# The output product of a recurrent mixer as two stacked float32r products instead of one fp32 product

## The chip, the cores and the metric

One core of a Trainium2 chip runs the whole program. The metric is the device time in microseconds of one execution. In what follows PE is the matrix engine (TensorE), DVE the vector engine, ACT the scalar engine, POOL GpSimd, SP the engine that issues most DMAs.

## The reference, cut to what matters

One transformer-like layer on x of shape (2, 1024, 512), with adaptive scales and shifts from a small product (mod). First a recurrent mixer (64 states), then a mixture of 32 experts (4 per token) with a shared expert of 1408 columns, both with a residual.

```python
h = layernorm(x) * (1 + ca) + sa
x_cat = jnp.roll(h, -512, axis=1)
x_shift = jnp.einsum('btd,ed->bte', x_cat, Wts) * g + h * (1.0 - g)
xn = layernorm(x_shift) * ln_w + ln_b
k = jnp.einsum('btd,sd->bts', xn, Wk)
v = jnp.einsum('btd,sd->bts', xn, Wv)
wkv = jnp.exp(-jnp.exp(time_first) * jax.nn.sigmoid(k)) * v
states[t] = states[t - 1] * jnp.exp(time_decay) + wkv[t]     # a scan over 1024 rows
out = jnp.einsum('bts,ds->btd', states, Wo)                  # the output product
x = x + ga * out
h2 = layernorm(x) * (1 + cb) + sb
x = x + gb * ffn(h2)        # router, top 4 of 32 experts, shared expert
```

## The kernel before, in words

The 2048 rows stand as NT = 16 tiles of 128 rows, eight for each of the two batches; a group is GT = 4 tiles (512 rows). Every engine has its own program, written out by hand in Python loops; the engines meet only in semaphores (`then_inc`, `wait_ge`), so an instruction that waits holds up everything that stands behind it on its engine.

The part in question is one loop, `for t in range(STEPS)`, of 22 steps, which each engine writes for itself. In step t:

- PE turns (transposes) the next tile of normalized rows (`turn(("h", t + 1))`), computes `mixer(t)`, a product of 12 float32r matmuls of 128x512 (L1640), then `project(t - 5)`, the output product of tile t - 5 (L1662), then turns `xn` and `h2` rows, and at t = 4, 8, 12, 16 computes `keys_values(g)` for group g = t / 4 - 1 (L1653). In steps 9 and 17, `project` stands at the step's end, in step 13 behind the first piece of shared-expert work. From step 10 on, pieces of the shared expert's first two chunks (L1690, L1702) fill in, and `router(g)` (L1673) at t = 9, 13, 17, 21.
- ACT takes turned tiles out of PSUM (hT rounded to float32r at L737, `xnT` at L742, `h2T` at L752), normalizes rows (L770, L787), prepares `kE` and `vV` for the scan (`decay_factor`, L810 to L813) and rounds the shared expert's operands (`xsH`, L860; `prodH`, L874).
- DVE adds and takes statistics (`mix_front` at L1151, `residual_sum` at L1164), forms the low halves of split operands (`h_lo` at L1058, `xsL` at L1214, `prodL` at L1224), and at the end of steps 4, 8, 12, 16 multiplies and scans (`kv_scan`, L1184 and L1187).
- POOL computes the reciprocal roots of the variances (`rsx`, `rsh`) and the row sums and scalings (L623 to L642).

A split operand is a float32 value as a rounded float32r part (H) and the rest (L), so that a sum of float32r products, H·H, H·L and L·H, gives nearly the float32 product. `mixer` and the shared expert do it so. `project` does not: it is one plain fp32 product of 64 rows (the 64 states) by 512 columns, which the compiled program runs as two matmul instructions. Its stationary operand is `states`, 64x512 for each of two groups in turn; its moving operand is `woT[:, b, :]`, the output weights scaled by the gate `ga` of batch b. Those are made once, in step 4: DVE scales `Wo` in eight instructions (`derive`, L1144) into `ho[:, 1, :]`, PE turns them (`("wo", b)`), ACT copies them out of PSUM (L728).

`project(t)` waits for `st_ok` of its group, given by the scan. The next group's scan takes the last state of the group before out of `states`. The "rows" turn of step 5 carries modulation vectors to HBM by way of `rowT`. The semaphores `t_full` and `t_taken` of the three PSUM banks for turns order PE against whoever takes a turned tile.

## Time and profile before

| what | value |
| --- | --- |
| runs, us | 720.56, 728.2, 723.08; median 723.08 |
| the profiled execution | 720.62 us, its span 718.8 us |
| mean granted TensorE clock | 0.976 |
| busy: PE, DVE, ACT, POOL | 672.5, 365.5, 288.6, 184.4 us |
| matmul instructions of the project product, L1662 | 32, 589 ns each |
| DMA | 118.27 MB, 165 GB/s on average |

The profile's times count from the start of the span. An idle time in square brackets is what an instruction's engine waited before it, with the instruction that released it. "issue" means that nothing in the profile is seen to have been waited for. A shape such as 64*128 64x512 gives the stationary operand (rows by columns) and the moving one. The mixer loop runs from about 28 to 235 us; behind it come routing, the experts and the rest of the shared expert.

### The profile page before, as it was taken

The page shows a single profiled execution, that of the slowest core. Times are in us where ns is not written, and L with a number is a line of the kernel's source. Part 1 is how long each engine was busy: PE and PEld are TensorE (multiplying, and loading weights), DVE is VectorE, ACT ScalarE, POOL GpSimd, SP SyncE. Part 2 cuts the span into 40 slices and gives each one's busy share as a digit, 9 for nine tenths or more (in the row PEclk, how much of TensorE's full clock was granted, in tenths as well). Part 3 has the DMA queues.
Part 4 walks back from the last instruction along what each step waited for, and adds up shares of the span by engine and source line. Part 5 has one row for each costly group of instructions (what it writes and reads, how often), then busy time and mean ns, then how long its engine had stood idle before and what let it go on. Part 6 is the DMA issues. An engine that isn't in the chain of part 4 may idle for free.

```text
span 718.8 us, 8895 instructions
## 1 busy us (share of the span) xinstructions
PE 672.5 (94%) x3218; PEld 467.9 (65%) x3218; DVE 365.5 (51%) x714; ACT 288.6 (40%) x552; POOL 184.4 (26%) x174
## 2 busy tenths in 40 slices
PE   4898788999998899998999899999999999999997
PEld 3665456768576667887665566666666666667875
DVE  3768759679687887763124223122122243225755
ACT  3444775656656543323234224233232343323231
POOL 1254465554627200000112122222221222120000
PEclk9799987999999999999999999999999999999999
DMA  7760200000223006305777877778899787816311
GB/s 276 243 238 1 76 15 30 16 30 18 85 77 116 29 1 232 134 1 206 267 235 231 291 229 261 249 234 282 270 324 338 239 273 258 284 23 234 117 50 69
DMA packets 50295, 118.27 MB, mean 165 GB/s; under 512 B 6904, under 2 KB 11084, under 8 KB 50252
## 3 DMA queue, kind: packets, MB, share of 16 engines
q1 hardware_dynamic: 45388, 109.31, 43.0%
q0 software_dynamic: 4864, 8.40, 5.4%
q8 instruction: 26, 0.43, 0.2%
q14 instruction: 17, 0.14, 0.1%
HBM read 100.87 MB, written 18.91 MB: 167 GB/s over the span
## 4 chain that ended last, share of the span: by engine, by line
PE 61%; DVE 5%; DMA 3%; ACT 2%; issue 2%; POOL 2%; SPq 0%; DVEq 0%; ACTq 0%; POOLq 0%
PE bank L1690 28%; PE bank L1702 11%; PE bank L1745 11%; PE bank L1762 6%; DMA egu<-in_L_ffn_Wu_dram 1%; PE bank L1733 1%; ACT xsH L860 1%; DMA xg<-h_rows,slot_tok 1%; PE bank L1793 1%; PE bank L1751 1%; DVE xres L1260 1%; DVE prodL L1224 1%; POOL ho L634 1%; DVE prod L1222 1%; POOL xres L642 1%
## 5 line engine op out<-in xcount | busy, mean ns | idle before, releaser
L1690 PE MATMUL bank<-xsH,wguH 128*128 128x512 f32 x352 | 144.1, 409 | 1.5 <-DVE xsL L1214 1.1
L1690 PE MATMUL bank<-xsL,wguH 128*128 128x512 f32 x352 | 138.9, 394 | 0.0
L1690 PE MATMUL bank<-xsH,wguL 128*128 128x512 f32 x352 | 138.6, 394 | 0.0
L1690 PEld LDWEIGHTS bank<-xsH,wguH 128*128 128x128 f32 x352 | 67.0, 190 | 25.5 <-issue 10.9
L1222 DVE TENSOR_TENSOR prod<-bank,silu 128x512 f32<-128x512 f32 x38 | 26.2, 690 | 111.2 <-PE bank L1690 87.7
L1745 PE MATMUL bank<-egu,xeT 128*64 128x352 f32 x512 | 79.3, 462 | 3.1 <-DMA egu<-in_L_ffn_Wu_dram 2.6
L1702 PE MATMUL bank<-wdH,prodH 128*128 128x512 f32 x176 | 73.7, 419 | 6.4 <-DVE prodL L1224 4.2
L692 POOL DMA_INDIRECT expert_sums<-ye,slot_to x32 | 49.4, 1543 | 115.7 <-DMA expert_sums<-ye,slot_to 91.5
L1690 PEld LDWEIGHTS bank<-xsL,wguH 128*128 128x128 f32 x352 | 66.9, 190 | 14.8
L1690 PEld LDWEIGHTS bank<-xsH,wguL 128*128 128x128 f32 x352 | 66.8, 190 | 13.2 <-issue 0.7
L699 POOL DMA_INDIRECT xg<-h_rows,slot_tok x16 | 16.8, 1053 | 219.8 <-DVE slot_w L1368 90.0
L874 ACT ACTIVATE prodH<-prod 128x512 fp32r<-128x512 f32 x38 | 24.0, 632 | 114.8 <-DVE prod L1222 114.8
L1702 PE MATMUL bank<-wdH,prodL 128*128 128x512 f32 x176 | 68.9, 391 | 0.0
L1702 PE MATMUL bank<-wdL,prodH 128*128 128x512 f32 x176 | 68.8, 391 | 0.0
L1745 PEld LDWEIGHTS bank<-egu,xeT 128*64 128x64 f32 x512 | 36.2, 137 | 42.2 <-issue 35.4
L868 ACT ACTIVATE silu<-bank 128x512 f32<-128x512 f32 x44 | 26.3, 598 | 71.9 <-PE bank L1690 70.5
L1248 DVE TENSOR_TENSOR xres<-ytmp,xres 128x512 f32<-128x512 f32 x44 | 30.0, 691 | 45.9 <-ACT ytmp L911 45.6
L1640 PE MATMUL bank<-wtsH,hT 128*128 128x512 f32 x128 | 49.1, 447 | 4.5 <-DVE mx L1151 3.1
L1702 PEld LDWEIGHTS bank<-wdH,prodH 128*128 128x128 f32 x176 | 33.1, 188 | 23.8 <-issue 7.4
L1214 DVE TENSOR_TENSOR xsL<-h2T,xsH 128x512 fp32r<-128x512 f32 x64 | 44.9, 746 | 4.8 <-ACT xsH L860 4.7
L1383 DVE TENSOR_TENSOR eprod<-bank,esilu 128x352 f32<-128x352 f32 x16 | 8.4, 525 | 75.0 <-ACT esilu L884 75.0
L1762 PE MATMUL bank<-ed,epT 128*64 128x512 f32 (+1 forms) x192 | 44.8, 600 | 0.8 <-issue 0.8
(222 smaller groups left out, 1019.8 us busy)
## 6 DMA issues: line engine op xcount, KB each, us to landing
egu<-in_L_ffn_Wg_dram SPq DMA_DIRECT2D x32, 704.0 KB, 6.0
egu<-in_L_ffn_Wu_dram SPq DMA_DIRECT2D x32, 704.0 KB, 7.5
ed<-in_L_ffn_Wd_dram SPq DMA_DIRECT2D x32, 512.0 KB, 5.3
h2T<-in_L_wmod_dram SPq DMA_DIRECT2D x6, 1024.0 KB, 8.9
ed<-in_L_ffn_Wd_dram SPq DMA_DIRECT2D x32, 192.0 KB, 6.3
h_rows<-ho SPq DMA_DIRECT2D x16, 256.0 KB, 2.0
expert_sums<-ye SPq DMA_DIRECT2D x16, 256.0 KB, 8.8
out_dram<-xres SPq DMA_DIRECT2D x16, 256.0 KB, 2.2
```

What stands on the lines that cost most here:

```text
L692: gp.indirect_dma_start(sums_dram[:, :], bass.IndirectOffsetOnAxis(slot_to[0:n, e, j:j + 1], axis=0), ye[0:n, :], None, bounds_check=B * T ...
L699: gp.indirect_dma_start(xg[:, :], None, h2_dram[:, :], bass.IndirectOffsetOnAxis(slot_tok[:, j:j + 1], axis=0)).then_inc(xg_in, 16)
L868: a.activation(silu[:, :], gB[:, :], ACT.Silu).then_inc(silu_ok, 1)
L874: a.activation(prodH[f][:, :], src[:, :], ACT.Copy).then_inc(phi_ok, 1)
L1214: v.tensor_tensor(xsL[:, c, :], h2T[:, g, c, :], xsH[:, c, :].bitcast(F32), ALU.subtract).then_inc(xlo_ok, 1)
L1222: v.tensor_tensor(to[:, :], uB[:, :], silu[:, :], ALU.mult).then_inc(prod_ok, 1)
L1248: v.tensor_tensor(xres[:, i, :], taken(p, g, m)[:, :], xres[:, i, :], ALU.add).then_inc(x_acc, 1)
L1640: ins = mm.matmul(s_bank[k][:, :], l[:, c, :], r[:, c, :], start=(n == 0), stop=(n == 3 * C - 1))
L1690: ins = mm.matmul(bk[:, :], l[f][:, w, c, :], r[:, c, :], start=(k == 0), stop=(k == 3 * C - 1))
L1702: ins = mm.matmul(dB[m % 2][:, :], l[f][:, m * P:(m + 1) * P], r[f][:, :], start=(f == 0 and k == 0), stop=(f == nf - 1 and k == 2))
L1745: ins = mm.matmul(bk[side, 0:F], xeT[:, c, side], egu[:, e, w, c, :], start=(c == 0), stop=(c == C - 1))
L1762: ins = mm.matmul(eyB[side, :], epT[0:n, c, side], ed[0:n, e, c, :], start=(c == 0), stop=(c == len(FC) - 1))
```

## The change

The states of a group are kept in `kE`, where the scan now writes in place. ACT rounds them into rows 0 to 63 of a new tile `sHL` (`states_hi`); DVE puts the rest into rows 64 to 127 (`states_lo`), and only that gives `st_ok`. The output weights stand twice, in rows 0 to 63 and again in 64 to 127: DVE's scaling writes each 64 columns twice, PE turns 128 columns instead of 64, ACT rounds the result into `woH`, and DVE puts the rest into `woL` (`wo_lo`). `project` is then two float32r products of 128 rows: `sHL` by `woH`, and `sHL` by `woL`, so all four cross terms are summed. The last state of a group goes to `wcol[:, 3:4]` with a copy at even groups. `rowT` loses its own memory and lies in `vV`, so ACT's "rows" copy waits for the first scan, and `decay_factor(1)` for the DMA out of it.

```diff
-            states_all = sb("states", [P, 2, GW], F32, pa)
-            woT = sb("woT", [S, B, H], F32, pa)
+            with ExitStack() as opening:
+                partial = sb("partial", [P, 2, GW], F32, opening)
+            sHL = sb("sHL", [P, 2, GW], F32R, pa)
+            woH = sb("woH", [P, B, H], F32R, pa)
+            woL = sb("woL", [P, B, H], F32R, pa)
...
-        woS = ho[:, 1, :].rearrange("p (c b s) -> p c b s", c=C, b=B)
+        woS = [ho[:, 1 + b, :] for b in range(B)]
+        rowT = vV[0:B * KINDS * C, 0:P]
...
                     elif kind == "wo":
-                        a.activation(woT[:, t[1], :], src[0:S, :], ACT.Copy).then_inc(t_taken[k], 1)
+                        a.activation(woH[:, t[1], :], src[:, :], ACT.Copy).then_inc(wo_hi, 1)
                     elif kind == "rows":
-                        a.activation(rowT[:, :], src[0:B * KINDS * C, 0:P], ACT.Copy).then_inc(t_taken[k], 1)
+                        act.wait_ge(st_full, 1)
+                        a.activation(rowT, src[0:B * KINDS * C, 0:P], ACT.Copy).then_inc(t_taken[k], 1)
...
+                    if g == 1:
+                        act.wait_ge(vrows_out, 16)
...
+                def states_hi(g):
+                    act.wait_ge(st_full, g + 1)
+                    a.activation(sHL[0:S, g % 2, :], kE[:, :], ACT.Copy).then_inc(st_hi, 1)
...
                     for q in before_mixer(t):
                         take(q)
+                    if scan_group(t - 1) is not None:
+                        states_hi(scan_group(t - 1))
...
                         for c in range(C):
-                            v.tensor_scalar(woS[:, c, b, :], woN[:, c, :], dcol[:, b, K_GA, c:c + 1], None, ALU.mult).then_inc(wo_scaled, 1)
+                            v.tensor_scalar(woS[b][:, c * P:(c + 1) * P].rearrange("p (a s) -> p a s", a=2),
+                                            woN[:, c:c + 1, :].to_broadcast([P, 2, S]), dcol[:, b, K_GA, c:c + 1], None,
+                                            ALU.mult).then_inc(wo_scaled, 1)
...
                     link(v.tensor_tensor(kE[:, :], vV[:, :], kE[:, :], ALU.mult))
-                    if g:
-                        dve.wait_ge(st_ok, g)
-                    v.tensor_tensor_scan(states[:, g % 2, :], wcol[:, 0:1].to_broadcast([S, GW]), kE[:, :],
-                                         states[:, 0, GW - 1:GW] if g % 2 else 0.0, ALU.mult, ALU.add).then_inc(st_ok, 1)
+                    v.tensor_tensor_scan(kE[:, :], wcol[:, 0:1].to_broadcast([S, GW]), kE[:, :],
+                                         wcol[:, 3:4] if g % 2 else 0.0, ALU.mult, ALU.add).then_inc(st_full, 1)
+                    if g % 2 == 0:
+                        dve.wait_ge(st_full, g + 1)
+                        link(v.tensor_copy(wcol[:, 3:4], kE[:, GW - 1:GW]))
+
+                def states_lo(g):
+                    dve.wait_ge(st_hi, g + 1)
+                    v.tensor_tensor(sHL[S:2 * S, g % 2, :], kE[:, :], sHL[0:S, g % 2, :].bitcast(F32),
+                                    ALU.subtract).then_inc(st_ok, 1)
+
+                def wo_lo(b):
+                    k, _ = turn_at[("wo", b)]
+                    dve.wait_ge(wo_hi, b + 1)
+                    v.tensor_tensor(woL[:, b, :], bank[k][:, :], woH[:, b, :].bitcast(F32), ALU.subtract).then_inc(t_taken[k], 1)
...
                     if 1 < t + 1 < NT:
                         h_lo(t + 1)
+                    if scan_group(t - 1) is not None:
+                        states_lo(scan_group(t - 1))
...
                     if t == 4:
                         derive_gb()
+                        wo_lo(0)
+                        wo_lo(1)
...
-                    mm.matmul(s_bank[k][:, :], states[:, g % 2, i * P:(i + 1) * P], woT[:, t // BT, :],
-                              start=True, stop=True).then_inc(s_full[k], 1)
+                    mm.matmul(s_bank[k][:, :], sHL[:, g % 2, i * P:(i + 1) * P], woH[:, t // BT, :], start=True, stop=False)
+                    mm.matmul(s_bank[k][:, :], sHL[:, g % 2, i * P:(i + 1) * P], woL[:, t // BT, :],
+                              start=False, stop=True).then_inc(s_full[k], 1)
```

DVE before, at the end of step 4 and the start of step 5, behind the first scan (`dcol` are vectors for the gate of the second half, `hT` is the low half of the next mixer operand, `neg` and `nb` are small vectors, `mx` is the sum with the mixer product):

```order
L1127 TENSOR_TENSOR dcol<-tmpc 128x4x2
L1132 RECIPROCAL dcol<-dcol 128x4x2
L1058 TENSOR_TENSOR hT<-bank,hT 128x512
L1051 TENSOR_TENSOR neg<-mv,neg_one 128x4
L1053 TENSOR_TENSOR nb<-neg,rs 128x4
L1151 TENSOR_TENSOR mx<-bank,mx 128x512
```

DVE now, the same place:

```order
L1135 TENSOR_TENSOR dcol<-tmpc 128x4x2
L1140 RECIPROCAL dcol<-dcol 128x4x2
L1209 TENSOR_TENSOR woL<-bank,woH 128x512 x2
L1066 TENSOR_TENSOR hT<-bank,hT 128x512
L1203 TENSOR_TENSOR sHL<-kE,sHL 64x512
L1059 TENSOR_TENSOR neg<-mv,neg_one 128x4
L1061 TENSOR_TENSOR nb<-neg,rs 128x4
L1161 TENSOR_TENSOR mx<-bank,mx 128x512
```

Two subtractions for the output weights (`woL`) stand ahead of `hT`, and the low half of the states (`sHL`) behind it, all of them ahead of `mx`.

DVE before, at the third scan, from the end of step 12 into step 13 (`kE` is the input of the scan, `st` a statistic of `mx`):

```order
L1184 TENSOR_TENSOR kE<-vV,kE 64x512
L1187 SCALAR_TENSOR_TENSOR states<-wcol,kE 64x512
L1058 TENSOR_TENSOR hT<-bank,hT 128x512
L1151 TENSOR_TENSOR mx<-bank,mx 128x512
L1153 BN_STATS st<-mx 128x6
```

DVE now, the same place:

```order
L1194 TENSOR_TENSOR kE<-vV,kE 64x512
L1195 SCALAR_TENSOR_TENSOR kE<-wcol,kE 64x512
L1199 COPY wcol<-kE 64x1
L1066 TENSOR_TENSOR hT<-bank,hT 128x512
L1203 TENSOR_TENSOR sHL<-kE,sHL 64x512
L1161 TENSOR_TENSOR mx<-bank,mx 128x512
L1163 BN_STATS st<-mx 128x6
```

A one-column copy follows the scan (at the first and third scan alone), and the low half of the states stands between `hT` and `mx` (at the first three scans; at the last there is no `hT` and no `mx` behind it).

ACT before, around the last scan, at the end of step 16 and in step 17 (`kE` and `vV` prepare the scan, `h2T` is the router's operand, `xsH` the shared expert's):

```order
L810 ACTIVATE kE<-bank,kvbias 64x512
L811 ACTIVATE vV<-bank,kvbias 64x512
L813 ACTIVATE kE<-kE,wcol 64x512
L752 ACTIVATE h2T<-bank,dcol 128x128 x4
L860 ACTIVATE xsH<-h2T 128x512 x4
```

ACT now:

```order
L812 ACTIVATE kE<-bank,kvbias 64x512
L813 ACTIVATE vV<-bank,kvbias 64x512
L815 ACTIVATE kE<-kE,wcol 64x512
L819 ACTIVATE sHL<-kE 64x512
L754 ACTIVATE h2T<-bank,dcol 128x128 x4
L866 ACTIVATE xsH<-h2T 128x512 x4
```

The rounded half of the states, which waits for DVE's scan, now stands ahead of `h2T` and `xsH`. The line numbers of the changed kernel run up to 26 higher than those of the kernel before.

## Rows read from the trace of the kernel before

**Rows 1.** The page's first part: busy time of each engine, share, instructions.
```profile
PE 672.5 (94%) x3218; PEld 467.9 (65%) x3218; DVE 365.5 (51%) x714; ACT 288.6 (40%) x552; POOL 184.4 (26%) x174
```

**Rows 2.** Timeline, PE, step 11: start us, us, line, operation, count, [idle before].
```profile
134.10 0.39 PE L1640 MATMUL bank<-wtsH,hT 128*128 128x512 f32 x1
134.41 1.12 PE L1662 MATMUL bank<-woT,states 64*128 64x512 f32 x2
135.47 0.50 PE L1690 MATMUL bank<-xsH,wguH 128*128 128x512 f32 x1
135.80 0.39 PE L1690 MATMUL bank<-xsH,wguL 128*128 128x512 f32 x1
136.03 0.40 PE L1690 MATMUL bank<-xsL,wguH 128*128 128x512 f32 x1
```

**Rows 3.** Timeline, DVE: end of step 4, start of step 5.
```profile
63.65 1.40 DVE L1144 TENSOR_SCALAR ho<-ho,dcol 128x64 f32<-128x64 f32 x8
...
66.92 0.68 DVE L1184 TENSOR_TENSOR kE<-vV,kE 64x512 f32<-64x512 f32 x1
...
67.64 1.22 DVE L1187 TENSOR_TENSOR_SCAN states<-wcol,kE 64x512 f32<-64x512 f32 x1
...
68.78 0.13 DVE L1130 COPY modc<-bank 128x8 f32<-128x8 f32 x1
...
70.10 0.64 DVE L1058 TENSOR_TENSOR hT<-bank,hT 128x512 fp32r<-128x512 f32 x1
```

**Rows 4.** Timeline, PE: project product of step 5.
```profile
68.96 1.09 PE L1662 MATMUL bank<-woT,states 64*128 64x512 f32 x2
```

**Rows 5.** Timeline, three engines, steps 6 to 8: the relay from row to row.
```profile
78.55 0.68 DVE L1151 TENSOR_TENSOR mx<-bank,mx 128x512 f32<-128x512 f32 x1
...
94.56 0.29 ACT L776 ACTIVATE nbh<-negh,rsh 128x1 f32<-128x1 f32 x1 [1.05 <-POOL rsh L606]
...
97.93 0.69 DVE L1058 TENSOR_TENSOR hT<-bank,hT 128x512 fp32r<-128x512 f32 x1 [3.81 <-ACT hT L737]
```

**Rows 6.** Timeline, steps 8 to 10, DVE and then PE.
```profile
108.27 1.24 DVE L1184 TENSOR_TENSOR kE<-vV,kE 64x512 f32<-64x512 f32 x1 [4.30 <-ACT kE L813]
...
121.10 3.79 DVE L1214 TENSOR_TENSOR xsL<-h2T,xsH 128x512 fp32r<-128x512 f32 x4 [0.78 <-ACT xsH L860]
...
123.74 0.52 PE L1690 MATMUL bank<-xsH,wguH 128*128 128x512 f32 x1 [0.69 <-DVE xsL L1214]
```

**Rows 7.** Windows: us, PE, PEld, DVE, ACT, POOL busy, PEclk, DMA, GB/s.
```profile
124.00:128.00 4.00, 4.00 (x14) 3.07 (x14) 3.80 (x10) 0.71 (x2) 0.00 (x0) 0.57 0.17 63
128.00:149.00 21.00, 21.00 (x99) 15.82 (x98) 13.59 (x31) 11.60 (x25) 13.13 (x13) 1.00 0.07 26
```

**Rows 8.** Timeline, steps 12 to 16: DVE, then PE twice.
```profile
157.63 1.22 DVE L1187 TENSOR_TENSOR_SCAN states<-wcol,kE 64x512 f32<-64x512 f32 x1
...
158.95 1.09 PE L1662 MATMUL bank<-woT,states 64*128 64x512 f32 x2 [0.16 <-issue]
...
190.67 0.50 PE L1702 MATMUL bank<-wdH,prodH 128*128 128x512 f32 x1 [0.89 <-DVE prodL L1224]
```

**Rows 9.** Timeline, step 17 to step 20: ACT, DVE, PE.
```profile
199.07 1.50 ACT L752 ACTIVATE h2T<-bank,dcol 128x128 f32<-128x128 f32 x4 [0.26 <-PE bank L1591]
200.66 2.20 ACT L860 ACTIVATE xsH<-h2T 128x512 fp32r<-128x512 f32 x4
...
201.32 2.50 DVE L1214 TENSOR_TENSOR xsL<-h2T,xsH 128x512 fp32r<-128x512 f32 x4 [0.48 <-ACT xsH L860]
205.01 0.69 DVE L1164 TENSOR_TENSOR xres<-bank,xres 128x512 f32<-128x512 f32 x1 [1.18 <-PE bank L1662]
...
224.79 0.50 PE L1702 MATMUL bank<-wdH,prodH 128*128 128x512 f32 x1 [1.37 <-DVE prodL L1224]
```

**Rows 10.** Groups by line, DVE: busy us, mean ns | idle before.
```profile
L1224 DVE TENSOR_TENSOR prodL<-prod,prodH 128x512 fp32r<-128x512 f32 x38 | 26.3, 692 | 26.5 <-ACT prodH L874 26.5
...
L1224 DVE TENSOR_TENSOR prodL<-silu,prodH 128x512 fp32r<-128x512 f32 x6 | 7.9, 1324 | 7.4 <-ACT prodH L874 7.4
```

More of the change, by code:

```diff
@@ L152, in build @@
             dcol = sb("dcol", [P, B, KINDS, C], F32, pa)
-            rowT = sb("rowT", [B * KINDS * C, P], F32, pa)
             tmpc = sb("tmpc", [P, 3, C, B], F32, pa)
@@ L181, in build @@
         rows = ho[0:24, 2, 2 * P:3 * P]
+        rowT = vV[0:B * KINDS * C, 0:P]
         kvN = mx[:, 1, :]
         kvT = mx[:, 2, :].rearrange("p (c m) -> p c m", c=C)
-        partial = states_all
-        states = states_all[0:S, :, :]
         LOT, NHOT = 8, 5
@@ L258, in build @@
          vef_ok, vex_ok, veh_ok, rsf_ok, rsx_ok, rsh_ok, dve_self, pool_self,
-         vrows_out, ab_in, cb_in, sb_in, rg_in, gate_in) = sems(
+         vrows_out, ab_in, cb_in, sb_in, rg_in, gate_in, wo_hi, st_full, st_hi) = sems(
              "rows_zero const_ok cols_in kv_in wo_in wr_in stage_in0 stage_in1 stage_in2 "
@@ L265, in build @@
              "vef_ok vex_ok veh_ok rsf_ok rsx_ok rsh_ok dve_self pool_self "
-             "vrows_out ab_in cb_in sb_in rg_in gate_in")
+             "vrows_out ab_in cb_in sb_in rg_in gate_in wo_hi st_full st_hi")
         (w_in, w_read, sg_exp, rb_ok, shift_ok, ex_ok, pos_full, mask_ok, scan_ok, route_ok,
@@ L500, in _ @@
                 turn_taken(sp, ("rows",))
-                sp.dma_start(rows_dram, rowT[:, :]).then_inc(vrows_out, 16)
+                sp.dma_start(rows_dram, rowT).then_inc(vrows_out, 16)
                 sp.wait_ge(vrows_out, 16)
@@ L779, in norm_out @@
                         act.wait_ge(wo_scaled, B * C)
-                    elif t == 1:
-                        turn_full(act, ("wo", 1))
-                    elif t == 2:
-                        act.wait_ge(part_full, len(VECTORS))
+                    elif t <= B:
+                        turn_full(act, ("wo", t - 1))
                     else:
@@ L1573, in turn @@
                         pe.wait_ge(wo_scaled, (t[1] + 1) * C)
-                        src, dst = [woS[:, c, t[1], :] for c in range(C)], dst[0:S, :]
+                        src = [woS[t[1]][:, c * P:(c + 1) * P] for c in range(C)]
                     else:
```

## The prediction

> **What bounds the kernel now.** I read the page's first part, then the timelines of PE and DVE side by side from 60 us to 240 us, since every touched instruction runs there. PE is busy 94% of the span [rows 1], which invites the conclusion that any time taken off PE comes off the kernel. For this stretch the reader should see that it is only sometimes so, and the waits tell where.
>
> Steps 4 to 9 (about 58 to 115 us) are a relay: DVE forms a row's statistics, POOL its rstd, ACT normalizes, ACT rounds the next hT, DVE subtracts, and only then does DVE take the next mixer product. in steps 7 and 8 ACT waits 1.05 us for POOL's rsh and DVE 3.81 us for ACT's hT [rows 5], and POOL had waited for DVE. PE follows: its products are ready before DVE takes them. At steps 8 to 10 the relay runs through ACT's kE into an unbroken DVE row (kE, the scan, hT, mx, xres, wguL, wdL, xsL), and PE waits 0.69 us for xsL [rows 6]. From 128 to 149 us PE is busy 21.00 of 21.00 us [rows 7]: here it is the bound. From the scan at 157.63 us DVE is again nearly unbroken, until PE waits 0.89 us for prodL at 190.67 [rows 8]. In steps 17 to 20 PE waits 1.37 us for a prodL [rows 9], which goes back over ACT and POOL to the DVE row that starts at 205.01 us. Behind 240 us nothing touched is left, so a shift there is carried to the end unchanged.
>
> **What leaves PE.** Sixteen project products of two fp32 passes each. In step 11 the last mixer product starts at 134.10 us and the first product behind the project at 135.47: 1.37 us, of which 0.23 is the mixer product's own step (135.80 to 136.03), leaving 1.14; the first product behind also takes 0.33 instead of 0.23 until its follower starts. So a project costs 1.24 us of PE's row [rows 2]. The two float32r products in its place are of the form whose step is 0.23 us, so 0.46 us, and 0.78 us is saved, if PE is the bound there. I take float32r over sHL and woH as the same form as the shared products over xsH and wguH (128 rows, 512 columns).
>
> "FP8 and Floating Point Precision" of the Trainium skill (TensorE Precision Notes) counts true fp32 as four passes. By it and the 0.23 us step of these rows the old product would be 0.92 us and the saving 0.46; the row shows 1.24, since the project also starts late and delays its follower, and the row decides.
>
> **What DVE gets**, each piece between instructions that the relay already waits for:
> - Step 4, scaling of Wo: eight instructions of 128 columns for eight of 64, which took 1.40 us, 0.18 each; one of 8 columns takes 0.13 [rows 3], so most is fixed. Between 0 and 1.4 us more; I take 0.3.
> - Two woL subtractions from PSUM, like the hT subtraction of 0.64 us [rows 3]: 1.3 us, in front of h_lo of step 5.
> - The copy of the last state at groups 0 and 2: about 0.13 us [rows 3], plus the wait for the scan's end where the follower used to overlap it: 0.3 us each, between 0.2 and 0.5.
> - Four states_lo, 64x512 with two inputs in SBUF, like kE: 0.68 us at 66.92, 1.24 at 108.27 [rows 3, 6]. I take 0.7, and 1.24 as the other end.
> - ACT gets four states_hi, like one xsH: a quarter of 2.20 us, 0.55 [rows 9]. DVE's states_lo waits for it.
>
> **Steps 4 and 5.** Scale 0.3, copy 0.3, woL 1.3, states_lo 0.7: 2.6 us more before DVE takes mixer product 5 (it stands right behind the hT of 70.10 us and two small ones [rows 3]). states_hi is hidden here under DVE's small instructions and woL. PE is hit too: project 0 started at 68.96 [rows 4] and now waits for states_lo, which ends near 73.5. Behind that wait stand mixer product 6 and the turn of xn 4; they come some 4 us late. DVE takes product 6 near 81.2 (78.55 plus 2.6 [rows 5]), and a late start at 75.6 with twelve products of 0.23 to 0.43 us ends between 78.6 and 81, so this stays hidden, if barely. I carry +2.6 through the relay to step 8; the projects of steps 5 to 8 give nothing, because PE waits after each.
>
> **Steps 8 to 10.** DVE's row gets states_lo, and before it the wait for ACT: st_full, 0.55 us of states_hi, then 0.7, of which hT hides 0.6. Net +0.9 before mx 9, and everything up to xsL at 121.10 is back to back. ACT's xnT and h2T also stand behind states_hi, but ACT waits for POOL's rstd just behind them, which has the same 0.9 us to come. The saved 0.78 of projects 4 and 5 only makes PE wait longer for xsL. +0.9.
>
> **Steps 11 and 12**: PE is the bound; two projects, 2 x 0.78 = -1.6.
>
> **Steps 13 to 16.** Copy 0.3, states_lo with its wait 0.9 less 0.1: +1.1 on DVE's row from 157.63 to 190.67. PE also waits for states_lo at project 8 (it started at 158.95, 0.1 us behind the scan [rows 8]): some +1.0 there. The four projects of steps 13 to 16 then save 3.1 us on PE, which turns the 0.89 us wait at 190.67 into about 3. +1.1.
>
> **Step 17.** states_hi now stands in front of h2T and xsH on ACT and waits for the scan's end at 200.84 (201.32 less the wait of 0.48), so xsH, which began at 200.66, begins near 203.0, and xsL, its pursuer, ends about 2.4 us later, near 206.2 instead of 203.8. (From 200.84: 0.55 of states_hi, then the 1.50 of h2T, which used to be done from 199.07 on.) DVE had waited 1.18 us for project 12 at 205.01 [rows 9]; that wait vanishes and the row starts at 206.2: +1.2. The later projects again only lengthen PE's wait.
>
> **Sum**: 2.6 + 0.9 - 1.6 + 1.1 + 1.2 = +4.2 us. The profiled execution took 720.6 us (718.8 of span, 1.8 around it), so 724.8 for it. It lies 2.5 us under the median 723.1 of the runs shown; from the median the forecast is 727.3.
>
> **Rivals.**
> - *PE decides everywhere* (faster). If the eleven projects from step 10 on all come off, and the DVE pieces fall in gaps: 11 x 0.78 = 8.6 us, 714.5. For it: PE's 94% [rows 1] and the gapless 21 us [rows 7]. Against: the three waits of PE for DVE in [rows 6, 8, 9], each at the end of a row to which DVE work is added. 0.08.
> - *The pieces are absorbed.* DVE is busy 51% overall [rows 1], and waits like 3.81 us [rows 5] look like room. If steps 4 to 8 absorb the 2.6: 723.1 + 4.2 - 2.6 = 724.7; if all is absorbed and PE's gain of 1.6 is left, 721.5. Against it: the waits are for ACT and POOL, which wait for DVE's earlier instruction, so the gap moves with it. 0.17.
> - *PE's clock* (slower). At 124 to 128 us the granted clock is 0.57 of full on average [rows 7], so mostly the 1.2 GHz level, where a product's step of 0.23 us about doubles, to 0.43; just before, PE had waited for xsL [rows 6]. The change makes PE wait more (4.5 us at step 5, 1.5 at 13, 3 at 16). Half clock costs nothing while PE waits anyway; it decides once two or three such stretches of 3.4 us fall where PE is the bound, as after 128 us [rows 7]: 1.7 us each, 3.4 to 5.1, so 730.7 to 732.4. 0.12.
> - *POOL holds DVE up* (slower). The same prodL takes 0.69 us late in the kernel and 1.32 beside POOL's row work [rows 10], so 1.24 for each states_lo: +0.5 x 4, 729.3. 0.13. "SBUF — State Buffer" of the Trainium skill (SBUF: two separate sides) says that a DVE instruction with two SBUF inputs and a GpSimd one exclude each other for a whole instruction; that speaks against this change, since states_lo is of that kind. By it each collision may cost a POOL instruction's whole length; the trace agrees in kind, with 1.32 for 0.69.
>
> **How the numbers follow.** The forecast, with sizes as above, has 0.50: 725 to 730. Predicted time: 727.3. Range 720 to 732: it takes in the absorbed case, POOL and the lower part of the clock case, and leaves out PE deciding everywhere and the worst of the clock. One per cent, 7.2 us, is about what a measurement can tell from no change: the three runs before lie 7.6 us apart. Faster by over 1% (under 715.8) 0.08, slower by over 1% (over 730.3) 0.16, within 0.76.
>
> **What the profile after would show.** Right: PE idle of 4 us or more before the first woH product, released by states_lo; project products of 0.39 us each; xsL and prodL still ending PE's waits, longer than before at 190 us; step 17's xsH behind states_hi. Wrong: mixer product 6 or xnT ending DVE's or ACT's waits in steps 6 and 7 (then step 5 costs over 2.6 us), no wait for prodL in step 16 (then DVE was no bound and the projects count), or states_lo near 1.24 us. What would overturn the sign is slack in the relay that I have not seen.

## The result and the profile after

The changed kernel takes 732.5 us (median of 4 runs, 731.1 to 734.6) where the kernel before takes 723.6 beside it on the same chip: ratio 1.0137, 95% interval 1.0105 to 1.0169. It is slower by 9.9 us by that ratio; the forecast was +4.2 us, and 732.5 lies half a microsecond outside the range. The changed kernel was run and timed three times more, with ratios 1.0104, 1.0105 and 1.0110. All 23 runs have a median of 731.1 us, the 34 of the kernel before beside them 722.7, so 8.4 us. I take 8 us as the effect: the direction is as forecast, the size double. One timed execution of an experiment, the cheap product alone, took 1099 us at a granted clock of 0.557 and is left out of that kernel's ratio.

The page of the kernel after, its first part [rows 1]:

```profile
PE 667.5 (92%) x3218; PEld 473.9 (65%) x3218; DVE 368.7 (51%) x722; ACT 290.8 (40%) x556; POOL 183.6 (25%) x174
```

PE lost 5.0 us of work, DVE gained 3.2 and ACT 2.2, and the span grew from 718.8 to 729.4 us. So PE's idle time grew by 15.6 us. The rest of the section says where.

**The product is as cheap as forecast.** Timeline of PE after, step 11 [rows 2]:

```profile
137.11 0.39 PE L1665 MATMUL bank<-wtsH,hT 128*128 128x512 f32 x1
137.34 0.39 PE L1687 MATMUL bank<-woH,sHL 128*128 128x512 f32 x1
137.57 0.39 PE L1688 MATMUL bank<-woL,sHL 128*128 128x512 f32 x1
137.79 0.39 PE L1716 MATMUL bank<-xsH,wguH 128*128 128x512 f32 x1
```

From 137.34 to 137.79 the project takes 0.45 us of PE's row, for the 1.24 of before.

**Steps 4 and 5.** Timeline of DVE after [rows 3], then of PE [rows 4]:

```profile
62.46 1.66 DVE L1152 TENSOR_SCALAR ho<-ho,dcol 128x128 f32<-128x128 f32 x8
...
66.72 1.22 DVE L1195 TENSOR_TENSOR_SCAN kE<-wcol,kE 64x512 f32<-64x512 f32 x1
67.97 0.14 DVE L1199 COPY wcol<-kE 64x1 f32<-64x1 f32 x1
...
69.50 1.24 DVE L1209 TENSOR_TENSOR woL<-bank,woH 128x512 fp32r<-128x512 f32 x2
70.65 0.68 DVE L1066 TENSOR_TENSOR hT<-bank,hT 128x512 fp32r<-128x512 f32 x1
71.36 0.69 DVE L1203 TENSOR_TENSOR sHL<-kE,sHL 64x512 fp32r<-64x512 f32 x1
```

```profile
69.31 0.40 PE L1665 MATMUL bank<-wtsH,hT 128*128 128x512 f32 x1
72.15 0.47 PE L1687 MATMUL bank<-woH,sHL 128*128 128x512 f32 x1 [2.44 <-DVE sHL L1203]
```

The scaling takes 1.66 us for 1.40; woL 1.15 from start to the start of hT; the low half of the states 0.69. PE waits 2.44 us for it. The mixer product ahead ran at half clock here, so it ended late; in the three further executions of the same kernel the same wait is 4.06 or 4.07 us.

**Step 9**, which I had dismissed. Timeline after, ACT, then PE and DVE [rows 6 stop just ahead of this place]:

```profile
112.28 0.63 ACT L819 ACTIVATE sHL<-kE 64x512 fp32r<-64x512 f32 x1 [2.01 <-DVE kE L1195]
...
113.30 1.48 ACT L754 ACTIVATE h2T<-bank,dcol 128x128 f32<-128x128 f32 x4
...
114.83 1.10 PE L1699 MATMUL bank<-wrN,h2T 128*128 128x34 f32 x8 [2.07 <-ACT h2T L754]
...
116.98 0.69 DVE L1174 TENSOR_TENSOR xres<-bank,xres 128x512 f32<-128x512 f32 x1 [1.42 <-PE bank L1688]
```

The same place before:

```profile
108.56 3.66 PE L1673 MATMUL bank<-wrN,h2T 128*128 128x34 f32 x32
109.23 1.51 ACT L752 ACTIVATE h2T<-bank,dcol 128x128 f32<-128x128 f32 x4
113.30 0.69 DVE L1164 TENSOR_TENSOR xres<-bank,xres 128x512 f32<-128x512 f32 x1
```

Read the rows of after from the bottom up: DVE waits 1.42 us for PE's project; PE had waited 2.07 for h2T with the last eight router products, which stand ahead of that project in step 9; h2T stands on ACT behind states_hi, and ACT had waited 2.01 for the scan. Before, ACT began h2T ahead of the scan (109.23 against 109.54), the router's 32 products followed each other without a gap, and DVE took xres without a wait.

**Step 13.** Timeline after, ACT, DVE and PE [rows 8]:

```profile
159.82 1.22 DVE L1195 TENSOR_TENSOR_SCAN kE<-wcol,kE 64x512 f32<-64x512 f32 x1
...
161.07 0.63 ACT L819 ACTIVATE sHL<-kE 64x512 fp32r<-64x512 f32 x1 [1.47 <-DVE kE L1195]
161.07 0.15 DVE L1199 COPY wcol<-kE 64x1 f32<-64x1 f32 x1
161.52 0.69 DVE L1066 TENSOR_TENSOR hT<-bank,hT 128x512 fp32r<-128x512 f32 x1 [0.30 <-DVE wcol L1199]
162.25 0.68 DVE L1203 TENSOR_TENSOR sHL<-kE,sHL 64x512 fp32r<-64x512 f32 x1
162.96 0.69 DVE L1161 TENSOR_TENSOR mx<-bank,mx 128x512 f32<-128x512 f32 x1
163.03 0.47 PE L1687 MATMUL bank<-woH,sHL 128*128 128x512 f32 x1 [2.35 <-issue]
```

DVE's hT and mx of before, behind the scan at 157.63:

```profile
158.77 0.66 DVE L1058 TENSOR_TENSOR hT<-bank,hT 128x512 fp32r<-128x512 f32 x1
159.35 0.67 DVE L1151 TENSOR_TENSOR mx<-bank,mx 128x512 f32<-128x512 f32 x1
```

From the scan's start to hT it is 1.70 us (159.82 to 161.52) instead of 1.14 (157.63 to 158.77), so the copy costs 0.56: its 0.15, the 0.30 of wait behind it, and the end of the scan that hT used to overlap. From hT to mx it is 1.44 instead of 0.58, so the low half of the states costs 0.86. PE waits 2.35 us; the profile names no releaser, but the product starts just behind the end of sHL (162.93).

What followed in this execution is in the windows of the kernel after (columns as in [rows 7]):

```profile
163.50:177.20 13.70, 13.70 (x56) 12.64 (x55) 7.79 (x29) 6.50 (x15) 6.44 (x6) 0.50 0.05 19
```

For 13.7 us TensorE ran at 1.2 GHz while busy throughout. The window of before, at full clock and with PE as busy:

```profile
160.00:180.00 20.00, 20.00 (x111) 16.15 (x110) 17.98 (x49) 13.09 (x28) 9.59 (x9) 1.00 0.05 20
```

The half clock reaches the relay by the router's products, for whose result ACT waits ahead of xsH (in each pair the first row is from before, the second from after):

```profile
160.90 1.87 PE L1673 MATMUL bank<-wrN,h2T 128*128 128x34 f32 x16
165.29 3.47 PE L1699 MATMUL bank<-wrN,h2T 128*128 128x34 f32 x16
165.98 0.28 ACT L818 ACTIVATE logits<-bank 128x136 f32<-128x136 f32 x1 [0.69 <-PE bank L1673]
174.77 0.28 ACT L824 ACTIVATE logits<-bank 128x136 f32<-128x136 f32 x1 [5.61 <-PE bank L1699]
167.14 4.22 DVE L1214 TENSOR_TENSOR xsL<-h2T,xsH 128x512 fp32r<-128x512 f32 x4 [0.40 <-ACT xsH L860]
175.92 2.50 DVE L1235 TENSOR_TENSOR xsL<-h2T,xsH 128x512 fp32r<-128x512 f32 x4 [5.56 <-ACT xsH L866]
```

From the project to the end of the router's products PE worked 11.5 us without a gap, where before it took 6.8. In three further executions of this kernel DVE's wait for xsH is 3.53, 1.92 and 0.32 us, with 6.8, 3.4 and 0 us of half clock between 160 and 180 us. So where the half clock falls here, PE is the bound and the half clock is paid.

**Steps 16 and 17.** Timeline of PE after, the wait that answers to 190.67 [rows 8], then ACT and DVE at the last scan [rows 9]:

```profile
198.93 0.50 PE L1728 MATMUL bank<-wdH,prodH 128*128 128x512 f32 x1 [1.62 <-DVE prodL L1245]
...
209.12 0.63 ACT L819 ACTIVATE sHL<-kE 64x512 fp32r<-64x512 f32 x1 [2.06 <-DVE kE L1195]
209.78 1.50 ACT L754 ACTIVATE h2T<-bank,dcol 128x128 f32<-128x128 f32 x4
...
211.37 2.20 ACT L866 ACTIVATE xsH<-h2T 128x512 fp32r<-128x512 f32 x4
...
212.03 2.50 DVE L1235 TENSOR_TENSOR xsL<-h2T,xsH 128x512 fp32r<-128x512 f32 x4 [1.55 <-ACT xsH L866]
...
214.44 0.68 DVE L1174 TENSOR_TENSOR xres<-bank,xres 128x512 f32<-128x512 f32 x1
```

ACT stood 2.06 us at the scan with h2T and xsH behind it, as forecast.

**Where the time goes, with four executions of the changed kernel and two of the one before.** The table gives the start of the same instruction, counted from the first product of keys_values(0) (59.55 us in the first profile of before), less its value there. "Again" is a second profile of the kernel before.

| start of | forecast | after 1 | 2 | 3 | 4 | before again |
| --- | --- | --- | --- | --- | --- | --- |
| mx, tile 5 | 2.6 | 3.03 | 2.62 | 2.63 | 2.63 | -0.01 |
| mx, tile 9 | 3.5 | 3.93 | 3.50 | 3.52 | 3.51 | -0.03 |
| xres, tile 4 (step 9) | 3.5 | 5.27 | 5.66 | 5.03 | 5.67 | 1.41 |
| keys_values(2) | 1.9 | 3.46 | 3.09 | 3.19 | 4.67 | 0.79 |
| mx, tile 13 | | 5.20 | 4.49 | 4.92 | 6.16 | 0.79 |
| keys_values(3) | 3.0 | 9.85 | 6.00 | 5.09 | 7.40 | 0.79 |
| xres, tile 12 (step 17) | 4.2 | 11.03 | 7.18 | 6.28 | 9.55 | 0.78 |
| end | 4.2 | 12.18 | 15.38 | 4.50 | 13.00 | 3.38 |

Up to tile 9 the executions agree within some 0.4 us, and three of four within 0.02. From there they spread with the stretches at half clock, and behind step 17 by several microseconds more, before as well. One execution is thus no measure of a term beyond tile 9; means are. At tile 12 the mean of the four is 8.5, of the two before 0.4: 8.1 us, near the 8.4 of all runs. At the end it is 9.6, from single executions that lie 11 us apart, so the agreement at tile 12 is in part luck.

### The profile page after: what moved, and what is told of

It is laid out like the page before. It is cut to its first block, busy times and chain, and to the rows that moved or that the text cites. A ratio compares the mean times of both kernels' runs of the same rounds, so it can differ in the third digit from the quotient of the medians.

```text
span 729.4 us, 8906 instructions
## 1 busy us (share of the span) xinstructions
PE 667.5 (92%) x3218; PEld 473.9 (65%) x3218; DVE 368.7 (51%) x722; ACT 290.8 (40%) x556; POOL 183.6 (25%) x174
## 4 chain that ended last, share of the span: by engine, by line
PE 59%; DVE 5%; DMA 3%; ACT 2%; issue 1%; POOL 0%; SPq 0%; DVEq 0%; ACTq 0%
PE bank L1716 27%; PE bank L1728 11%; PE bank L1771 11%; PE bank L1788 6%; DMA egu<-in_L_ffn_Wu_dram 1%; PE bank L1759 1%; ACT xsH L866 1%; DMA xg<-h_rows,slot_tok 1%; PE bank L1819 1%; PE bank L1777 1%; DVE xres L1281 1%; DVE xsL L1235 1%; PE bank L1699 0%; DVE prod L1243 0%; ACT ytmp L917 0%
## 5 line engine op out<-in xcount | busy, mean ns | idle before, releaser
L1771 PE MATMUL bank<-egu,xeT 128*64 128x352 f32 x512 | 81.0, 470 | 3.1 <-DMA egu<-in_L_ffn_Wu_dram 3.0
L1665 PE MATMUL bank<-wtsH,hT 128*128 128x512 f32 x128 | 47.0, 430 | 3.0 <-DVE mx L1161 2.4
L1235 DVE TENSOR_TENSOR xsL<-h2T,xsH 128x512 fp32r<-128x512 f32 x64 | 43.1, 720 | 11.0 <-ACT xsH L866 10.9
```

The lines of the kernel that those rows point to most:

```text
L1235: v.tensor_tensor(xsL[:, c, :], h2T[:, g, c, :], xsH[:, c, :].bitcast(F32), ALU.subtract).then_inc(xlo_ok, 1)
L1665: ins = mm.matmul(s_bank[k][:, :], l[:, c, :], r[:, c, :], start=(n == 0), stop=(n == 3 * C - 1))
L1771: ins = mm.matmul(bk[side, 0:F], xeT[:, c, side], egu[:, e, w, c, :], start=(c == 0), stop=(c == C - 1))
```

## The experiments

Sixteen runs were made, three of them of the changed kernel again and one of the kernel before. Ratios are against the kernel before on the same chip. "Marks" are differences as in the table above.

### Does PE's wait bring the half clock?

The kernel before, with the third scan's semaphore released only behind two spare subtractions on DVE:

```diff
+                def late_states():
+                    link(v.tensor_tensor(vV[:, :], kE[:, :], kE[:, :], ALU.subtract))
+                    v.tensor_tensor(vV[:, :], kE[:, :], kE[:, :], ALU.subtract).then_inc(st_ok, 1)
...
+                    if t == 13:
+                        late_states()
```

> The kernel before, unchanged but for the third scan: its result is released to PE only behind two spare 64x512 subtractions on DVE at the start of step 13 (1.4 us of DVE time), so that PE waits some 2 us ahead of the project product of step 13, as in the changed kernel; the products stay fp32. Theory A (a wait of PE in step 13 brings the granted clock down, and the router, xsH and xsL behind it come late): half clock for some 7 to 14 us from about 160 us, DVE waits several us for xsH in step 13/14, and the time is 4 to 7 us over the kernel before. Theory B (the clock has nothing to do with that wait, DVE's added time alone counts): +1.0 to +2.0 us. Theory C (it is the float32r products or the freed PE time that lower the clock): +1 to +2 us here too, clock unchanged.

Measured: 725.0 us, ratio 1.0039 (1.0002 to 1.0076). PE waits 2.18 us at project 8 (2.35 in the changed kernel), the mark of mx of tile 13 is 1.4 us over that of keys_values(2), and in the one profile the granted clock stays full from 127 to 342 us. In the marks a delay of this size on DVE costs about itself; in the run's time it is 2.8 us, with an interval from 0.1 to 5.5. Here, then, a wait of PE of this length did not bring the half clock.

The changed kernel, with that wait filled:

```diff
+                    if t == 8:
+                        for q in range(8):
+                            mm.matmul(s_bank[k][:, :], hT[:, 1, 0, q % C, :], wtsH[:, q % C, :], start=True, stop=True)
                     pe.wait_ge(st_ok, g + 1)
```

> The changed kernel with eight spare float32r products of 128x512 (1.8 us) that PE computes into the project's own bank ahead of its wait in step 13; they are overwritten. DVE and ACT are untouched. Theory A (the empty 2.35 us ahead of the product bring the clock down): the granted clock stays full after 160 us, DVE's 5.56 us wait for xsH falls to under 1 us, and the time is 4 to 6 us under the changed kernel's, about 727 us. Theory B or C: no change, or up to 0.5 us more.

> The changed kernel with eight spare products ahead of the wait at project 8, a second time, beside the changed kernel on the same chip. Theory A: again no half clock in 160 to 180 us, and the median some 2 us under that of the changed kernel. Theory B: the two medians within 1 us of each other or the filled one slower, and as much half clock between 150 and 250 us in one as in the other.

Measured: 733.3 us, ratio 1.0162 (1.0119 to 1.0204), and the second time 727.9, ratio 1.0094 (1.0058 to 1.0131). The windows of the second, from 160, 180 and 230 us:

```profile
160.00:180.00 20.00, 19.48 (x111) 16.27 (x111) 18.74 (x47) 11.57 (x24) 7.20 (x7) 1.00 0.07 27
180.00:230.00 50.00, 43.01 (x194) 33.22 (x192) 34.46 (x79) 28.88 (x58) 24.41 (x22) 0.93 0.26 90
230.00:252.00 22.00, 20.91 (x103) 17.17 (x104) 18.48 (x55) 12.97 (x24) 12.37 (x20) 0.92 0.13 48
```

There is no half clock behind project 8, but some behind 180 and behind 230. DVE's wait for xsH, 5.56 us in the first execution of the changed kernel, was 0.30 in the first profile with the wait filled, as theory A had it; the 4 to 6 us did not come. The changed kernel, run beside it:

> The changed kernel once more, unaltered, for a second profiled execution. Theory (the time beyond the relay's terms is a stretch at half clock in steps 13 and 14, as the profiles of the changed kernel and of its variant with the old product show it, and it recurs): about 10 us over the kernel before, the granted clock halved again somewhere in 160 to 180 us, and the marks of step 14 some 3.5 us later than the relay's terms put them. Rival (it was one execution's accident, and the rest lies behind 270 us): the same median, no half clock in 160 to 180 us, about 8 us at 235 us and the rest behind it.

> The changed kernel a third time, unaltered. Two profiled executions of it had the granted clock halved in 163 to 177 us and in 165 to 172 us, right behind PE's wait of 2 us for the low half of the states at project 8. Theory A (that wait is followed by the half clock): again half clock somewhere in 160 to 180 us, and step 14 1.4 to 3.5 us later than the relay's terms give. Theory B (the half clock falls where it falls): nothing there, as in the profile of the reordered kernel with step 9 alone.

> The changed kernel a fourth time, unaltered, for the count of profiled executions with the half clock behind project 8's wait. Theory A: half clock in 160 to 180 us. Theory B: none. Either way the median of all its runs stands firmer: 730.3 to 732.5 us is expected.

Measured: 730.3 us (1.0104; 1.0058 to 1.0150), 730.1 (1.0105; 1.0079 to 1.0132), 731.8 (1.0110; 1.0070 to 1.0151). The window from 160 to 180 us of the second, third and fourth execution (the granted clock is the third figure from the right):

```profile
160.00:180.00 20.00, 17.96 (x89) 15.51 (x88) 15.43 (x42) 9.90 (x20) 6.60 (x7) 0.83 0.07 27
```

```profile
160.00:180.00 20.00, 17.64 (x98) 15.27 (x97) 17.12 (x45) 11.17 (x24) 6.49 (x6) 0.91 0.07 27
```

```profile
160.00:180.00 20.00, 17.87 (x105) 14.99 (x104) 17.42 (x42) 12.44 (x25) 8.53 (x8) 1.00 0.07 27
```

And the project of step 13 moved behind the step's other work, so that PE does not wait at it:

```diff
-ROUTER_FIRST = (9, 17)
+ROUTER_FIRST = (9, 13, 17)
```

> The changed kernel with the project product of step 13 at the end of the step, behind the router's products, as it stands in steps 9 and 17 (ACT takes the logits one place earlier). PE no longer waits for states_lo in step 13. Theory A: the clock stays full after 160 us and 4 to 6 us come back, about 727 us; DVE's residual sum of tile 8 then waits for the late product, which can take up to 2 us of it back. Theory B: within 1 us of the changed kernel. Theory C: the same as the changed kernel.

Measured: 732.2 us, ratio 1.0133 (1.0078 to 1.0188). No gain. In its profile PE waits further on instead, 3.82 us for xsL at 179.56, and half clock stands from 180.65 to 184.06.

What follows: half clock stood between 160 and 180 us in three of four executions of the changed kernel (with the other kernels that have the open wait, in six of eleven), and in none of the four in which the wait is filled or gone (the fourth comes below). That speaks for a link, but weakly: one of those four is the kernel just shown, whose half clock begins 0.65 us behind the window. And the time did not follow: by the ratios the filled kernel is 0.8 to 1.2 us under the changed one on the same chip, and it was 1.8 us over the changed kernel's first ratio the time before, all inside the intervals; it got its half clock elsewhere. That PE's waits cost 3 or 4 us by way of the clock is neither shown nor excluded.

### PE's side alone

The kernel before, with the scan writing float32r states and two products of 64 rows; the low halves are left out:

```diff
-                    mm.matmul(s_bank[k][:, :], states[:, g % 2, i * P:(i + 1) * P], woT[:, t // BT, :],
-                              start=True, stop=True).then_inc(s_full[k], 1)
+                    mm.matmul(s_bank[k][:, :], sR[:, g % 2, i * P:(i + 1) * P], woT[:, t // BT, :], start=True, stop=False)
+                    mm.matmul(s_bank[k][:, :], sR[:, g % 2, i * P:(i + 1) * P], woT[:, t // BT, :],
+                              start=False, stop=True).then_inc(s_full[k], 1)
```

> The kernel before with the scan written as float32r and each fp32 project product replaced by two float32r products of 64 rows by 512; it leaves out the low halves of the states and of the weights (the second product repeats the first). DVE and ACT do what they did before. If the relay over DVE, ACT and POOL is the bound outside steps 11 and 12 (my forecast's reading): 1 to 3 us under the kernel before. If PE decides from step 10 on: 7 to 9 us under it. The granted clock should stay as it was, since PE's waits are where they were.

Measured: 723.0 us, ratio 0.9995 (0.9962 to 1.0028). Marks: -0.46 us at keys_values(2), -0.69 at xres of tile 12 (step 17). The cheap product by itself is worth nothing that can be measured, where I had expected 1 to 3 us; the interval, from 2.7 us under to 2.0 over, leaves most of that possible, and excludes the 7 to 9 us of PE deciding.

### The other side alone

The changed kernel's work on ACT and DVE, but the product as before, fp32 over the rounded 64 rows; the low halves are made and not used:

```diff
+                    mm.matmul(s_bank[k][:, :], sHL[0:S, g % 2, i * P:(i + 1) * P].bitcast(F32), woH[0:S, t // BT, :].bitcast(F32),
+                              start=True, stop=True).then_inc(s_full[k], 1)
```

> The changed kernel with all of its work on ACT and DVE, but with the output product of before: one fp32 product of the 64 rounded rows of sHL by those of woH. The low halves are made and not used, so they are left out of the result. Theory (products count only where PE is the bound, two of sixteen): 1.6 us more than the changed kernel, 734.1 us, ratio 1.0155. Rival one (nothing on PE counts, as the kernel with two float32r products of 64 rows suggests, with 0.7 us at most): 732.5 to 733.2 us. Rival two (from step 10 on each project counts in full): 8.6 us more, 741 us.

> The kernel with the states rounded behind the router's operand, but with the output product of before: one fp32 product of the 64 rounded rows of sHL by those of woH; the low halves are made and not used, so they are left out of the result. It gives what the cheaper product is worth when the relay is in this order. Theory (two projects in steps 11 and 12, where PE is the bound, at 0.78 each): 1.6 us more than that kernel, 727.3 us, ratio 1.007. Rival (the earlier row lets PE be the bound in more steps, and with PE busier the half clock also costs more): 3 to 5 us more, 729 to 731.

Measured: 736.5 us, ratio 1.0200 (1.0175 to 1.0225), 0.9% or 6 us over the changed kernel; in the other order of ACT (next experiment) 733.6, ratio 1.0136 (1.0089 to 1.0184), again 6 us over its partner. My theory of 1.6 us is refuted in the first order; the 3 to 5 us of the second text's rival are nearer. Marks: at keys_values(2) 6.30 and 3.90; at keys_values(3) 13.47 and 12.65. The second, from 160 to 183 us:

```profile
160.00:183.00 23.00, 20.96 (x77) 17.17 (x76) 14.58 (x38) 10.68 (x21) 7.35 (x7) 0.63 0.06 24
```

PE idles 2 us at project 8 and is then busy without a break, most of it at half clock: here it is the bound, up to step 15.

So the halves don't add up: products alone -0.4 us, DVE's and ACT's work alone +14.4, both together +8. The added waits make PE late; once it is late, its own products count. How much of the 6 us is the products' own length and how much the half clock is not told apart: in single profiles the old product costs 2.7 and 3.5 us up to keys_values(2), and behind it both of its profiles have 20.5 us of half clock, where the changed kernel's four have 3.4 to 13.7.

### ACT's order in steps 9 and 17

states_hi behind the takes of the turned tiles in both steps (and in step 17 behind xsH, with the low half behind xsL):

```diff
                     for q in before_mixer(t):
                         take(q)
-                    if scan_group(t - 1) is not None:
+                    if scan_group(t - 1) is not None and t not in (9, 17):
                         states_hi(scan_group(t - 1))
...
+                    if t in (9, 17):
+                        states_hi(scan_group(t - 1))
...
-                    if scan_group(t - 1) is not None:
+                    if scan_group(t - 1) is not None and t != 17:
                         states_lo(scan_group(t - 1))
...
                     if t == 17:
                         lo_group(0, g + 1)
+                        states_lo(3)
```

> The changed kernel with ACT's rounding of the states (states_hi) moved behind h2T in step 9 and behind h2T and xsH in step 17, and the low half behind xsL in step 17. Same computation. Theory (relay terms, two of them mis-sized): the router's operand no longer stands behind the wait for the scan, so the residual sum behind the router comes 1.3 us earlier or more, and step 17 no longer costs its 1.2 us; together 2.5 us less than the changed kernel, about 730.0 us, ratio 1.010. Rival (these waits are filled by others, or the time comes from PE's clock and from the end of the kernel, which no such order touches): 732.5 us, ratio 1.0135, with the mark at the router unchanged.

> The changed kernel with ACT's rounding of the states behind h2T in step 9 alone; step 17 stays as in the changed kernel. Same computation. Theory (the wait of the router in step 9 is the costlier of the two, and what follows from it in PE's rows): residual sum 4 comes as in the kernel with both moved, at +3.5 us over before, step 17 still costs 1.2 us, and the time lies 0.8 to 1.2 us over that kernel, near 726.7 us, ratio 1.0065. Rival (step 17 is what it was, or the gain was the clock's accident): 729 to 732 us.

> The kernel with the states rounded behind the router's operand in steps 9 and 17, and besides eight spare products ahead of the wait at project 8. Theory A: the 1.4 us that half clock at 163 to 170 us cost in the profile without the spare products are gone, and the median is 1 us or more lower, 724.5 us. Theory B: 725.7 us or up to 1 us more, the spare products being worth nothing.

Measured: both steps 725.7 us, ratio 1.0050 (1.0016 to 1.0084); step 9 alone 727.9, 1.0072 (1.0041 to 1.0104); both, with the wait at project 8 filled, 728.8, 1.0079 (1.0049 to 1.0109). The timeline of the first, step 9:

```profile
113.97 1.08 PE L1702 MATMUL bank<-wrN,h2T 128*128 128x34 f32 x8 [0.34 <-ACT h2T L754]
114.03 0.63 ACT L819 ACTIVATE sHL<-kE 64x512 fp32r<-64x512 f32 x1
...
117.41 0.69 DVE L1176 TENSOR_TENSOR xres<-bank,xres 128x512 f32<-128x512 f32 x1
```

PE's wait for h2T shrinks from 2.07 to 0.34 us and DVE's for the project is gone: xres of tile 4 stands at +3.50 to +3.54 in all three, where the changed kernel has 5.0 to 5.7. Xres of tile 12 stands at 3.89 to 4.43 instead of 6.3 to 11.0. Against the changed kernel's mean ratio of 1.0114 this takes off 4.6, 3.0 and 2.5 us, where I had expected 2.5 for both steps (beside the changed kernel on its own chip, step 9 alone takes off 2.3). Step 9 is the larger part; the 1.6 us between one step and both lie inside the intervals. What both steps leave over the kernel before, 3.6 us, is near the forecast without its term for step 17, 3.0. In step 17 the mark from keys_values(3) to tile 12 falls from 1.2 to 0.4, not to 0: PE now waits 0.77 us for the low half of the states. The spare products gave nothing in this order either.

### DVE's pieces

Without the two woL subtractions; the second product reads woH, so the weights' low half is left out:

```diff
-                        wo_lo(0)
-                        wo_lo(1)
```

> The changed kernel without the two subtractions that make the low half of the output weights (woL); the second product reads woH instead, so the weights' low half is left out of the result. Theory (each piece on DVE in the relay is carried unchanged): steps 4 and 5 cost about 1.6 instead of 3.0 us, so 1.4 us less than the changed kernel, 731.1 us. Rival (the relay absorbs pieces): 732.5 us as the changed kernel, and DVE takes mixer product 6 no earlier.

Measured: 730.0 us, ratio 1.0105 (1.0067 to 1.0143). The mark of mx of tile 5 stands at 1.41 instead of 2.62, and that of tile 9 at 2.28 instead of 3.50: in the profile the piece costs its 1.2 us until there. Behind it nothing of that is left: keys_values(2) stands at 4.05 and xres of tile 12 at 7.85, within what the changed kernel has. In the run's time it shows as 0.7 us, inside the intervals. So up to tile 9 the theory holds, and whether a piece taken off there shortens the whole is not shown.

The low half of the states on POOL, the copy of the last state on ACT, in the better order:

```diff
-                    v.tensor_tensor(sHL[S:2 * S, g % 2, :], kE[:, :], sHL[0:S, g % 2, :].bitcast(F32),
-                                    ALU.subtract).then_inc(st_ok, 1)
+                    gp.tensor_tensor(sHL[S:2 * S, g % 2, :], kE[:, :], sHL[0:S, g % 2, :].bitcast(F32),
+                                     ALU.subtract).then_inc(st_ok, 1)
...
+                    if g % 2 == 0:
+                        a.activation(wcol[:, 3:4], kE[:, GW - 1:GW], ACT.Copy).then_inc(st_hi, 1)
```

> The order of the kernel with the states rounded behind the router's operand, and besides the states' low half on POOL instead of DVE (four instructions), the copy of the last state on ACT. Same computation. Theory (DVE's own pieces in the relay are the cost): three low halves of 0.7 us and two copies with their waits of 0.3 to 0.5 come off DVE's row, 2.5 us less than with the reordering alone, about 727.5 us. Rival (POOL is in the relay too, and is slower at it): a POOL instruction of this kind takes 1.3 us for 128 rows, it stands ahead of the reciprocal root of the next row, and DVE with two operands in SBUF runs beside it; then nothing is won, 730 us or more, and the rstd of the row comes 1 us later at steps 5, 9 and 13.

Measured: 726.5 us, ratio 1.0062 (1.0036 to 1.0088), no better than the order alone, though its marks are lower: 2.49 at mx of tile 5 (2.61 with the order alone), 2.47 at tile 9 (3.49), 3.58 at xres of tile 12 (4.07). Its timeline in step 5, DVE and then POOL:

```profile
70.84 0.17 DVE L1154 TENSOR_TENSOR tmpc<-tmpc,modc 128x8 f32<-128x8 f32 x1
71.04 1.21 DVE L1155 TENSOR_TENSOR dcol<-tmpc 128x8 f32<-128x8 f32 x1
72.29 0.20 DVE L1160 RECIPROCAL dcol<-dcol 128x8 f32<-128x8 f32 x1
```

```profile
70.97 1.26 POOL L655 TENSOR_TENSOR sHL<-kE,sHL 64x512 fp32r<-64x512 f32 x1 [1.19 <-ACT wcol L837]
```

A DVE instruction of 8 columns, 0.17 us otherwise, lasts until POOL's subtraction ends. In step 5 DVE is rid of 0.7 us of work and gets 1.0 us of waiting in its place. The Trainium skill ("SBUF — State Buffer", SBUF: two separate sides) has a DVE instruction with two inputs in SBUF and a GpSimd one that reads SBUF exclude each other for a whole instruction; these rows agree with it.

### The kernel before again

> The kernel before once more, unaltered, for a second profiled execution. Its first one lay 2.5 us under the median of its runs. Theory (single executions differ by some 3 us behind 270 us, in the experts' part, whatever stands before): the marks up to 235 us agree within 0.7 us, and what differs lies behind 270 us. Rival (the clock's stretches move the mixer loop too): the marks up to 235 us differ by over 1.5 us.

Measured: 723.2 us, ratio 1.0001 (0.9977 to 1.0025). Its mark in step 9 lies 1.41 us off (half clock at the router's products, 111 to 118 us), 0.79 remains from step 12 on, and 2.6 us more come between 343 and 405 us. So the rival holds in part: the clock moves the mixer loop of the kernel before by about a microsecond, too.

No version beat the kernel before.

## Why the prediction missed, by its own steps

Means of the four executions of the table less the two of before, step by step; they add up to 8.1 us where the forecast's terms add up to 4.2. Of the 3.9 us between them, 1.1 lie in step 9, where the order on ACT was put at nothing, 0.5 in step 13 (0.3 of it the copy), and 1.9 between mx of tile 13 and keys_values(3), for which there was no term; the rest is 0.1 or 0.2 in each of three terms.

- **What leaves PE**: right in size (0.45 us for 1.24). The two products have the step of the shared products, as forecast.
- **Steps 4 and 5**: 2.6 forecast, 2.7 measured, with every piece near its estimate: scaling +0.26, woL 1.15, low half 0.69. The wait of PE for it, forecast at 4 us or more, was 2.44 in one execution and 4.06 or 4.07 in three. Nothing was absorbed up to tile 9, as forecast.
- **Steps 8 to 10**: +0.9 forecast, +0.9 measured before tile 9. Behind it failed the sentence "ACT's xnT and h2T also stand behind states_hi, but ACT waits for POOL's rstd just behind them". It asks when ACT is free, not who waits for h2T. In step 9 that is PE with the router, and the project stands behind the router. Measured: +1.1 on the mean (1.8 in the changed kernel, 0.7 in that of before), and removing this order took off 1.5 to 2.2 us at the mark. I had priced the same order in step 17 and not here.
- **Steps 11 and 12**: -1.6 forecast, -1.5 on the mean. The four executions give 1.0 to 2.6, so the agreement is of the mean alone.
- **Steps 13 to 16**: +1.1 forecast, +1.6 up to tile 13. The copy was mis-sized, 0.56 for 0.3, since behind its 0.15 DVE waits another 0.30; the low half took 0.86 for 0.8. Then another +1.9 up to keys_values(3), which no term had; all four executions have half clock in this part, and lose 0.2 to 4.7 us in it. The forecast had DVE's row as the bound here. In the three executions with half clock there, PE was, from its wait at project 8 to the end of the router's products, so that a late start and half clock were both paid. "The four projects of steps 13 to 16 then save 3.1 us on PE, which turns the 0.89 us wait at 190.67 into about 3": it was 1.62, 1.77 and 2.00 with half clock ahead of it, and 3.28 in the execution without.
- **Step 17**: +1.2 forecast, +1.4 measured, of which 2.1 in the execution with half clock up to 202 us and 1.2 in the others.
- **Rival PE's clock**, given 0.12: it named a price of 1.7 us a stretch where PE is the bound and a total of 730.7 to 732.4. The median of all runs, 731.1, is there, and so are the stretches in steps 13 to 16 (+1.9 us), but step 9's term is another 1.1 of the miss, and filling one of the waits did not bring time back. It holds in part.
- **Rival POOL**: wrong for the states' low half on DVE. All four took 0.68 or 0.69 us, in each of four executions. But POOL runs nothing beside any of them, so that a collision costs nothing is not what they show. It came when the work was put on POOL.
- **Rival PE decides everywhere**: refuted by the cheap product in the kernel before, -0.4 us (2.7 at most). But its contrary, which I had used for the sum (a project counts in two of sixteen steps), is refuted too, by the 6 us that the old product costs in the changed kernel.

With 731.1, the median of all runs, the range would just hold, and the change would still be double the forecast. The range failed since it was built round a sum of terms that were each read in the schedule of before. The width for what the clock does was put into one rival and left out at its upper end.

Open: what brings the half clock. Between keys_values(2) and tile 15 the profiles of the changed kernel have 3.4 to 13.7 us of it and those of before 0 and 3.4. But the kernels with the old product have 20 with little idle time of PE there (2.8 and 4.3 us), and the one with POOL's subtraction has none with 11.4 us of idle time. The sum of PE's waits alone does not sort them, and the single wait at project 8 is followed by half clock in six profiles of eleven.

## What to carry to other kernels

Where a new wait is put at the head of an in-order engine, list everything behind it up to the next wait that would have been as long, and for each item ask who takes it and what stands behind that one; the missed item here (h2T for the router, the router ahead of the project) was two engines away. Savings on one engine and costs on another don't add: price the saving in the schedule as it will be once the costs have made that engine late. And when executions of one kernel agree within 0.02 us up to a point and spread behind it, take terms from one profile up to there and from several beyond.

## What the runs showed that I had not expected

- The mixer loop repeats to 0.02 us in three of four executions up to tile 9, then spreads by up to 4.8 us at step 17, with the stretches at half clock.
- A DVE instruction with 8 columns took 1.21 us for 0.17 beside a POOL subtraction of 1.26 us.
- The part behind 270 us, which nothing touches, differs between executions of the same kernel: 2.6 us between the two profiles of before.
